# Memory attention in a macaron block: rotation by DMA between partitions, and another order of a step

## The reference

```python
qkv = xn @ w_qkv                      # xn: layer norm of x
q, k, v = jnp.split(qkv, 3, axis=-1)  # each then B, heads, N, 64
qr, kr = (rope(q, pos), rope(k, pos))
def step(carry, inp):                 # one segment of 32 positions
    mem, z = carry
    q_s, k_s, v_s, qn_s, kn_s = inp   # qn, kn: without rotation
    scores = einsum('bhnd,bhmd->bhnm', q_s, k_s) * SCALE   # then causal mask
    sdpa = einsum('bhnm,bhmd->bhnd', softmax(scores), v_s)
    sq = elu1(qn_s)
    mem_out = (sq @ mem) / (sq @ z + 1e-06)
    out = beta * mem_out + (1.0 - beta) * sdpa
    sk = elu1(kn_s)
    prev_v = (sk @ mem) / (sk @ z)
    mem = mem + einsum('bhnk,bhnv->bhkv', sk, v_s - prev_v)
    z = z + sk.sum(axis=2)
    return ((mem, z), out)
```

## Time and profile before

| what | value |
|---|---|
| median of three runs | 2839.58 us |
| the profiled execution | 2842.93 us, its span 2840.8 us |
| busy share of the span: PE, DVE, ACT, POOL | 74%, 70%, 50%, 38% |
| this stage | about 298 to 1129 us of the span |
| its steps (L1725 to L1725) | 31 from 359.0 to 1128.6 us |

### The profile page before, as it was taken

One profiled execution on the slowest core, in us unless ns is written; L12 is line 12 of the kernel. 1 busy time (PEld: TensorE's weight loads), 2 busy tenths in 40 slices (PEclk: granted clock), 3 DMA queues, 4 the chain that ended last, 5 costly groups with the idle time before them and its releaser, 6 DMA issues. The chain is left out here.

```text
span 2840.8 us, 87273 instructions
## 1 busy us (share of the span) xinstructions
PE 2095.6 (74%) x35326; PEld 1682.5 (59%) x35326; DVE 1985.0 (70%) x4767; ACT 1418.4 (50%) x2385; POOL 1079.2 (38%) x873
## 2 busy tenths in 40 slices
PE   3687599999999997679398947656666545558894
PEld 2576478888888876568278946433222233336794
DVE  5787577777777775779664433889999966757443
ACT  1555234444444442447364522468988754436452
POOL 3656334455554442556365621000000122206563
PEclk7789699999999998679699975765555577868997
DMA  4132200000000000023413220000000000012324
GB/s 109 45 103 83 80 2 0 0 0 0 0 0 0 0 0 3 31 83 93 147 45 91 73 88 0 0 0 1 1 0 0 0 1 1 0 36 70 88 77 114
DMA packets 95266, 104.00 MB, mean 37 GB/s; under 512 B 18936, under 2 KB 81000, under 8 KB 94464
## 3 DMA queue, kind: packets, MB, share of 16 engines
q1 hardware_dynamic: 74416, 64.12, 8.3%
q0 software_dynamic: 18176, 37.79, 3.9%
q10 hardware_dynamic: 2512, 0.02, 0.0%
HBM read 60.00 MB, written 46.20 MB: 37 GB/s over the span
## 5 line engine op out<-in xcount | busy, mean ns | idle before, releaser
L2472 POOL TENSOR_TENSOR bw_kT<-b_knT,b_head_of 128x768 f32<-128x768 f32 x40 | 58.5, 1494 | 650.7 <-SPq L2295 493.6
L2269 DVE CUSTOM_DVE_ANT_0 be_logs<-be_joint,be_logs 128x1024 f32<-128x1024 f32 x256 | 293.3, 1220 | 7.5 <-ACT be_logs L2242 7.5
L2242 ACT ACTIVATE be_logs<-be_joint,b_tiny 128x1024 f32<-128x1024 f32 x256 | 281.0, 1117 | 10.0 <-PE be_joint L2212 3.4
L2212 PE MATMUL be_joint<-be_partsT_k,be_partsT_q 64*128 64x512 f32 x512 | 195.4, 767 | 93.4 <-DVE be_sums L2269 89.9
L405 POOL DMA_INDIRECT d_pairs<-s_y_tile,s_x_tiles x156 | 178.6, 1145 | 119.4 <-DVE s_y_tile L1293 94.9
L1600 POOL TENSOR_TENSOR m_roped_q<-m_raw_q,m_cos 128x1024 f32<-128x1024 f32 x32 | 75.9, 2373 | 371.7 <-ACT m_raw_q L1536 371.7
L2212 PEld LDWEIGHTS be_joint<-be_partsT_k,be_partsT_q 64*128 64x128 f32 x512 | 72.0, 278 | 215.8 <-DVE be_sums L2269 211.3
L405 POOL DMA_INDIRECT d_pairs<-g_y_tile,g_x_tiles x156 | 153.9, 986 | 97.5 <-ACT g_y_tile L828 73.1
L332 POOL DMA_INDIRECT d_rows<-g_xn,g_slot x128 | 131.7, 1029 | 80.0 <-DVE g_slot L323 43.6
L332 POOL DMA_INDIRECT d_rows<-s_xn,s_slot x128 | 128.9, 1007 | 73.6 <-DVE s_slot L323 37.3
L1142 PE MATMUL s_ps_y<-s_down,s_a_tile 128*128 x1248 | 151.8, 275 | 0.0
(11 more groups left out here) (464 smaller groups left out, 6338.4 us busy)
## 6 DMA issues: line engine op xcount, KB each, us to landing
g_x_tiles<-d_rows SPq DMA_DIRECT2D x78, 132.0 KB, 2.1
s_x_tiles<-d_rows SPq DMA_DIRECT2D x78, 132.0 KB, 2.1
d_rows<-d_rows SPq DMA_DIRECT2D x32, 132.0 KB
g_shared<-d_pairs SPq DMA_DIRECT2D x8, 512.0 KB, 7.4
g_xn<-d_pairs SPq DMA_DIRECT2D x8, 512.0 KB, 7.5
s_up_raw<-L_ffn_We SPq DMA_DIRECT2D x16, 256.0 KB, 5.3
s_down<-L_ffn_We SPq DMA_DIRECT2D x16, 256.0 KB, 5.8
s_up_raw<-d_pairs SPq DMA_DIRECT2D x8, 512.0 KB, 7.5
```

The source lines that it names most:

```text
L2212: last = nc.tensor.matmul(joint_ps[k % DEPTH][:, a, :], partsT[0][rows, b, i * P:(i + 1) * P], partsT[1][rows, b, half * 512:(half + 1) * ...
L2242: nc.scalar.activation(logs[k % DEPTH][:, :, :], joint_ps[k % DEPTH][:, :, :], ACT.Ln, bias=A.tiny[:, :]).then_inc(s.log_ready, 1)
L2269: nc.vector.tensor_tensor_reduce(out=flat, in0=joint_ps[k % DEPTH][:, :, :].rearrange("p a j -> p (a j)"), in1=flat, scale=1.0, scalar=0.0 ...
L2472: last = nc.gpsimd.tensor_tensor(kT[:, h, :, :], A.knT[:, bass.ds(j * GROUP, KEYS), :], A.head_of[:, h:h + 1].unsqueeze(2).broadcast_to([P ...
```

## The change

- `w_rot` and its set-up go, and with them the 16 matmuls a tile that projected the partner.
- The partner is made by data movement. VectorE multiplies the projection in PSUM by a sine table with a sign for odd partitions (`front_spin` into `spun`), and SyncE copies `spun` into `turned` with odd and even partitions exchanged: two DMAs of 64 partitions x 4 KB for the keys and two for the queries, each step. GpSimd adds as before, but does cos of keys, cos of queries, then both additions.
- Keys go through banks 1 and 3, queries through banks 0 and 2, and keys are done first. `project` writes bank 1 in place of a bank of `back_ps`.
- `scores(w)` moves from the end of step w-1 into step w, between `recall_q` and `additions`. So `softmax_1` stands after `back_o`, and `softmax_2`, `softmax_3` and `softmax_4` stand between and behind the two `back_mem`. `recall_q` waits for the product that read the bank, not for `u`.

```diff
+            def swap(f, k):
+                spun_sem, moved, roped_sem = ((s.q_spun, s.q_moved, s.q_roped), (s.k_spun, s.k_moved, s.k_roped))[k]
+                sp.wait_ge(spun_sem, at(f, 2, 2))
+                wait(sp, roped_sem, f)
+                sp.dma_start(turned[k][0::2, :, :], spun[k][1::2, :, :]).then_inc(moved, 16)
+                sp.dma_start(turned[k][1::2, :, :], spun[k][0::2, :, :]).then_inc(moved, 16)
...
                 fill(2 * half, w_qkv, 512 * half, s.q_full)
-                wait(pe, s.scores_read, f)
-                fill(2 * half + 1, w_rot, 512 * half, s.q_full)
...
             def scores(f):
-                wait_alone(pe, s.rope_done, at(f, 2, 2), s.passed)
+                wait(pe, s.x_done, f)
+                pe.wait_ge(s.q_roped, f + 1)
+                wait_alone(pe, s.k_roped, f + 1, s.passed)
...
             def recall_q(w, half):
-                wait_alone(pe, s.u_ready, at(w, 2, half + 1), s.passed)
+                if half == 0:
+                    pe.wait_ge(s.q_phi, w + 1)
+                wait_alone(pe, s.back_step, at(w, 8, 2 * half + 2), s.passed)
...
+                copy_phi(w)
                 soft_exp(w)
-                copy_phi(w)
                 if more:
-                    front(w + 1, 0)
-                    front(w + 1, 1)
+                    copy_raw(w + 1, 1)
+                    elu(w + 1, 1)
+                    copy_raw(w + 1, 0)
+                    elu(w + 1, 0)
...
+            def rope_cos(f, k):
+                copied, cos_sem = ((s.q_copied, s.q_cos), (s.k_copied, s.k_cos))[k]
+                pool.wait_ge(copied, at(f, 2, 2))
                 wait(pool, s.scores_full, f)
+            def rope_moved(f, k):
+                pool.wait_ge(moved, at(f, 32, 32))
...
+                for half in range(2):
+                    dve.wait_ge(copied, at(f, 2, half + 1))
+                    nc.vector.tensor_tensor(spun[k][:, 4 * half:4 * half + 4, :], front_ps[2 * half + k][:, :].rearrange("p (k t) -> p k t", t=P),
+                                            wide(signed_sin).broadcast_to([P, 4, P]), ALU.mult).then_inc(spun_sem, 1)
...
             def tile(w):
-                softmax_1(w)
+                if norm:
+                    norm_1(w + 2)
                 back_u(w, 0)
                 back_u(w, 1)
-                softmax_2(w)
                 back_o(w, 0)
                 back_o(w, 1)
+                softmax_1(w)
+                back_mem(w, 0)
+                softmax_2(w)
+                back_mem(w, 1)
+                softmax_3(w)
+                softmax_4(w)
                 if more:
-                    front_rope(w + 1, 0)
-                back_mem(w, 0)
-                if norm:
-                    norm_1(w + 2)
-                back_mem(w, 1)
+                    front_spin(w + 1, 1)
+                    front_spin(w + 1, 0)
+                    front_phi(w + 1, 1)
                 if norm:
                     norm_2(w + 2)
                 if more:
                     front_phi(w + 1, 0)
-                    front_rope(w + 1, 1)
-                if more:
-                    front_phi(w + 1, 1)
                 back_x(w)
```

More of the change, by code:

```diff
@@ L1379, in _, with tile @@
             sp.wait_ge(s.loaded, 16 * (LOADS - 1))
+            def swap(f, k):
[4 more added lines that the diff above has]
+                sp.dma_start(turned[k][1::2, :, :], spun[k][0::2, :, :]).then_inc(moved, 16)
+            def tile(w):
+                if not (isinstance(w, int) and w == TILES - 1):
+                    swap(w + 1, 1)
+                    swap(w + 1, 0)
+            swap(0, 1)
+            swap(0, 0)
+            in_tiles(sp, tile)
+            sp.wait_ge(s.k_moved, 32 * TILES)
+            sp.wait_ge(s.q_moved, 32 * TILES)
         @block.tensor
@@ L1481, in answers, with project @@
                 last.then_inc(s.back_full, 1)
-            def project(w):
+            def project(w, more):
+                if more:
+                    pe.wait_ge(s.k_copied, at(w + 1, 2, 1))
+                    pe.wait_ge(s.k_spun, at(w + 1, 2, 1))
+                else:
+                    pe.wait_ge(s.scores_read, w + 1)
                 pe.wait_ge(s.oT_ready, w + 1)
                 for k in range(PAIRS):
-                    last = nc.tensor.matmul(back_ps[:, 2, 0:D], oT[:, k, :], w_out[:, k, :], start=(k == 0), stop=(k == PAIRS - 1))
+                    last = nc.tensor.matmul(front_ps[1][:, 0:D], oT[:, k, :], w_out[:, k, :], start=(k == 0), stop=(k == PAIRS - 1))
                 last.then_inc(s.back_full, 1)
@@ L1493, in tile @@
                 recall_q(w, 0)
-                if more:
-                    fill_q(w + 1, 0)
                 recall_q(w, 1)
-                if more:
-                    fill_q(w + 1, 1)
+                scores(w)
                 additions(w, 0)
@@ L1507, in tile @@
                     fill_v(w + 1)
-                project(w)
-                if more:
-                    scores(w + 1)
+                project(w, more)
                 if more and not (isinstance(w, int) and w == TILES - 2):
                     turn_x(w + 2)
-            pe.wait_ge(s.set_up, 4)
+            pe.wait_ge(s.loaded, 16 * (LOADS - 1))
+            pe.wait_ge(s.set_up, 2)
             turn_x(0)
             for half in range(2):
+                fill_k(0, half)
+            for half in range(2):
                 fill_q(0, half)
-            for half in range(2):
-                fill_k(0, half)
             fill_v(0)
-            scores(0)
             turn_x(1)
@@ L1579, in _ @@
             copy_x(0)
-            front(0, 0)
-            front(0, 1)
+            for k in (1, 0):
+                copy_raw(0, k)
+                elu(0, k)
             copy_v(0)
@@ L1724, in back_x @@
                 dve.wait_ge(s.back_full, at(w, BACKS, 8))
[L1725 removed]
+                nc.vector.tensor_tensor(X[:, w, :], X[:, w, :], front_ps[1][:, 0:D], ALU.add).then_inc(s.x_done, 1)
             def tile(w):
```

108 lines of the change are left out of this document (56 added, 52 removed).

## The result

The changed kernel takes **2988.77 us** (2972.37 to 2997.78, 4 runs) against 2839.3 (2835.86 to 2841.23, 4 runs) before: a ratio of 1.0521, interval 1.0473 to 1.057. The sign was forecast, the size was not: +149 us where +77 stood, and 9 us outside the range.

What follows compares the result with a forecast made beforehand. TensorE was taken to bound the kernel before; the new step is a loop through VectorE and TensorE, 21.3 + 2.0 + 1.6 (collisions) + 2.5 (clock) = 27.4 us, net +77, giving 2917 us, range 2850 to 2980.

Steps and rivals of the forecast that it cites:

- The sign: Whole kernel: slower by over 0.2% at a chance of 0.78, faster 0.19, within it 0.03.
- 31 steps: 849.4: All 31 loop steps at 27.4 us each, against 769.6 in the trace before: 80 us more.
- An ordinary step: One loop step of the changed kernel: 21.3 + 2.0 + 1.6 + 2.5 = 27.4 us.
- The collisions: From S, start of softmax's maximum subtraction: VectorE's 1-beta product and m_exps scaling wait 2.0 and 1.6 us for GpSimd's cos products.
- the rival of 0.15: Softmax: the small product goes ahead of GpSimd, only the scaling waits; step 23.4 us, 2791 in all; chance 0.15.
- The clock: TensorE after 4.5 us idle: low clock adds 2.3 us to answers and 0.2 to fill_v a step, 2.5 in all.
- The loop without both: Loop through VectorE (12.6 us) and TensorE (8.7) without collisions or the clock's loss: 21.3 us a step.
- If the collisions don't count at all: Rival for the step: 21.3 us and 0.5 of clock, 2741 us in all; chance 0.04.
- What bounds the kernel before: The step is bound by TensorE, busy 554.23 of 600 us, its list nearly without a gap.
- If nothing else bound the step: Dropping the w_rot matmuls would then save some 4 us of the 24.8 us step, 130 us in all.
- The DMAs: Exchange of partners between partitions: 4 us a pair, costed at nothing, with 2 us to spare.
- Ahead of the first step: Before the loop 4 us go: four blocks with w_rot and the building of that tile, less the first DMAs.

Runs made afterwards that it cites:

- Run 4: The changed kernel with 32 small matmuls once ahead of TensorE's first block of projections: 2933.61 us, ratio 1.0331 to the kernel before.
- run 5: The changed kernel with 64 small matmuls once ahead of TensorE's first block: 3095.56 us, ratio 1.0506 to the kernel before.
- run 6: The kernel before with 32 small matmuls once ahead of TensorE's first block: 3320.47 us, ratio 1.1285 to the unshifted kernel before.
- Run 3: The changed kernel with twelve unused 128x128 matmuls a step in TensorE's idle time ahead of the answers: 2871.58 us, ratio 1.0109 to the kernel before.
- run 12: The rearranged kernel of run 10 with 8 small unused matmuls ahead of the wait for the softmax's transpose: 2777.78 us, ratio 0.9778 to the kernel before.
- run 10: Run 9 with keys' cos product first, keys' phi from PSUM, queries' phi before normalization, queries' addition after that phi: 2827.06 us, ratio 0.9945 to the kernel before.
- run 1: The changed kernel with GpSimd's cos products waiting until VectorE has done the same step's softmax scaling: median 2894.5 us, ratio 1.0096 to the kernel before.
- run 7: The changed kernel with the cos products on VectorE, read from PSUM, GpSimd keeping the two additions: 3024.65 us, ratio 1.0262 to the kernel before.
- run 8: The kernel before, old order, without the w_rot matmuls; the exchange of partners is left out of the result: 2954.75 us, ratio 1.0049 to the kernel before.
- run 2: The changed kernel without the DMAs between partitions; the exchange of partners is left out of the result: 2982.78 us, ratio 1.0508 to the kernel before.
- run 9: Run 7 with 32 small matmuls on the identity ahead of TensorE's first wait of the stage: 2849.05 us, ratio 1.0021 to the kernel before.

## Why the prediction was right and wrong

- **The term that was missing: the fetching of code.** The step that failed is "31 steps: 849.4", which took every step to be an ordinary one and put the fetching of TensorE's instructions at nothing, without a word on it. Six were 7 to 9 us longer, 53.5 in all with what follows them: that is the error in the profiled execution (its 2972.37 against a forecast of 2920 for it). The median run is 16 longer still; in runs without a profile these steps can't be counted, so that this is the number of long steps is likely and not shown. No row of before hinted at it. Runs 4 and 5 show that the code's place makes these steps come and go, and run 6 that this doesn't count against the change: by its code's place alone, the kernel before differs from itself by 12.8%.
- **An ordinary step: 27.4 forecast, 27.34 measured.** Run 4, where all steps are ordinary, has 857.6 for the 850.4 of the sum.
- **The collisions: 2.0 and 1.6 forecast, 1.88 and 1.91 measured,** in that order. GpSimd started at S + 2.39 (forecast 2.49) and the small product at S + 2.75 (2.85). Only in the long steps did the first collision fall the other way, the rival of 0.15.
- **The clock: 2.5 forecast; the two stretches are 2.9 longer.** The answers lost 2.1 (2.3) and the values 0.7, of which I had taken 0.2. Run 3 gave back 1.8 of it on average; run 12 gave 1.9, against run 10.
- **The loop without both: 21.3 forecast,** and 27.34 - 1.88 - 1.91 - 2.9 = 20.7 by what was measured. Its sum holds a slip: TensorE's named terms (7.03, 0.73, 0.74 and one 0.1) are 8.6, not 8.7. The terms that came out too high and too low nearly cancel; that the 27.4 is better than its parts is luck. Nor could 21.3 be had by taking the collisions away: runs 1 and 7 ended at 24, because the same locks moved to VectorE's tail. The rival "If the collisions don't count at all" (2741) was not reached by either of these edits.
- **What bounds the kernel before: half right.** TensorE was busy nearly all of the time, but in a loop through both engines, and run 8 shows that without `w_rot` the step stays at 24.15 at best. About 22.8 of it is that loop and 1.3 the low clock in its gap, so with the clock held the shorter list alone would give some 1.4 us (24.24 less 22.8, an estimate) of the 4.25. The sentence "If nothing else bound the step" was the right caution; I never worked out the loop of the old order, and so couldn't say what a shorter list alone would give there.
- **The DMAs: costed at nothing, rightly.** 2.3 and 2.4 us each instead of 4 for a pair; the additions ended at 708.47, with the scores some 5 us later. The keys' pair was ready 2.97 us behind its first issue (700.25 to 703.22). That is near the estimate of 3.2 from the Trainium skill's 2.0 us and 436 GB/s ("DMA: Bandwidth & Descriptors", section "Anatomy of one DMA — SWDGE (gpsimd) path"), which the page fits to DMAs issued by GpSimd; these were issued by SyncE. The Trainium skill's rule against two transfers of half the partitions (same page, section "Rules for kernel authors") had no price here, as run 2 shows.
- **Ahead of the first step: -4 forecast, -4.8 measured.**

## What to carry to other kernels

When a loop's body is long, compare kernels with their loops' code in more than one place: look for instruction packets in the loop, and shift the code by some tens of instructions before a few per cent are credited to an edit. Ahead of taking work from the busiest engine, work out the longest loop through two engines as well: its gaps may be filled by the very work that goes. A lock between GpSimd and VectorE was not removed by moving one of the two (runs 1 and 7: it went to the next operation); it nearly went where VectorE's input came from PSUM and GpSimd's addition stood beside such work (run 10). After each such edit the clock has to be read again: a gap that opens can take back, at the low clock, part of what the work that left it gave (run 8).

## What the runs showed of the hardware

- **A loop's code may be fetched again or not, by its place.** 32 matmuls ahead of the loop of before make every step of it fetch, at 12 us a step; none or 64 of them, and no step in the steady part does. The changed kernel fetches in six steps with none, in no step of the steady part with 32, in eight with 64. The Trainium skill tells of such fetching ("Runtime: NRT & Kernel Launch", section "Instruction fetch mechanics"): instructions come in blocks of 16 KiB, and a branch to a target outside of the current window of two blocks forces a fetch. The traces agree in that the longest pause lies at the turn of the loop (5.53 and 7.72 us) and in the packets' size. The page gives two blocks as 512 instructions, and all that TensorE keeps as 2048, or 128 KiB. A step here has 1594 matmuls and loads as the traces count them, or 1530 after the change: by the window it would be fetched every time, by the 2048 it would fit. Neither is what the runs show, and the nine packets of a long step are 147 KB, more than the 128 KiB. The measurement decides; why some trips through the loop fetch and others don't stays open.
- **The normalization waits too.** L1657, a tensor_scalar on 128x128 out of SBUF with two numbers a partition, took 2.37 us in place of 0.34 beside GpSimd's addition (run 7), as long as that addition. The prediction had only operations on two tiles in mind.
- **A gap of 0.74 us, two outcomes.** In run 10 that gap stood ahead of the answers, and the clock was 0.50 some 2 us later; with eight matmuls in it (run 12) the clock was 0.98 over the stage. The gap alone does not decide it. In run 9 it stands ahead of the answers in each step, and the values that follow take 3.78 in one step and 1.98 in the next:

```profile
750.75 3.78 PE L1431 MATMUL m_front<-m_w_qkv,m_xnT 128*128 128x512 f32 x4
774.92 1.98 PE L1431 MATMUL m_front<-m_w_qkv,m_xnT 128*128 128x512 f32 x4
```

And in run 12 some steps fall to the low level in the values with no gap ahead of the answers at all. What tells such steps apart stays open, and so does whether the added work or the missing gap held the clock in the others.
